# Last stage of a two-layer graph network: own values as transposes, ranks by one maximum, and the edge product moved from GpSimd to VectorE

## The chip, the cores and the metric

One Trainium2 chip, one of its cores. The metric is the device time of one launch in microseconds (us), the median of several runs.

## What is computed

A node table x of 50,000 rows by 256 features goes through two graph layers. The edges are 25,000 random pairs plus one self loop for each node. The first layer is a two-layer perceptron with a batch norm and a degree-weighted sum over edges. The second is attention with 8 heads of 32 features over the same edges:

```python
h = jnp.maximum(_layernorm(x, axis=-1), 0.0)
q = (x @ Wq + bq).reshape(n, DH, H) * scaling
k = (x @ Wk + bk).reshape(n, DH, H)
v = (x @ Wv + bv).reshape(n, DH, H)
s = jnp.einsum('edh,edh->eh', q[row], k[col])
m = jax.ops.segment_max(s, row, num_segments=n)
e = jnp.exp(s - m[row])
z = jax.ops.segment_sum(e, row, num_segments=n)
a = e / z[row]
out = jax.ops.segment_sum(a[:, None, :] * v[col], row, num_segments=n)
return out.reshape(n, -1) @ Wo + bo
```

`x` in the five lines for q, k and v is `h`, and the result is added to x. All arrays are fp32.

## The kernel before

The kernel runs in stages, each a loop over 98 tiles of 512 nodes (`TILE`; 128 partitions by 4 rows, `ROWS`). The stages ahead sort the edges, compute the first layer, and write q, k, v, the scores of the self loops and the weights that go with them to tables. The change lies in the last stage, whose names begin with `e_`, and in a constant made at the start.

In the last stage every tile has at most 512 slots for its true edges. For each tile GpSimd gathers the far node's keys and values (`e_kv`, four indirect DMAs of 128 rows), and SyncE loads the tile's own values (`e_mine`), queries (`e_q`), self state (`e_state`) and rows of x (`e_x`). A one-hot matrix from slots to nodes, `hot_h`, is built by VectorE (L2290), turned by TensorE (L2228), and widened to fp32 by ScalarE. With it TensorE spreads the queries over the slots (L2256), brings scores to the nodes (L2265) and attention weights back to the slots (L2244). A slot's place among the edges of its node is its rank. It is found with a product by the upper triangle `before_h` (L2232) and four multiply-and-add instructions (L2335), and `e_layer` holds it as a one-hot of 8.

The attention-weighted mean is accumulated in `e_mean_ps`, in two halves of the features (`kc`), for four rows each: the gathered values times their weight (L2138, GpSimd) by `hot` (L2216), and the own values times theirs (L2191, ScalarE, 32 instructions of one row and head) by the fp32 identity (L2218). An fp32 matmul written once in the code stands twice in the trace. ScalarE copies the mean out (L2183), TensorE multiplies by the output weights (L2204, L2206), VectorE adds x (L2282), and SyncE stores.

Each engine runs its own program over a ring of tiles (`over_ring`). In turn i, `at(l)` is tile i - l, so that in one turn TensorE works on tile i (turn, prefix, queries), i-1 (scores), i-2 (edge weights), i-3 (mean) and i-4 (output). The order within a turn is written out by hand, and the engines meet at semaphores alone. TensorE's order is: turn and prefix, first half of the output (`product(at(4), 0)`), `mean(at(3), 0)`, second half of the output, edge weights, `mean(at(3), 1)`, queries, scores. VectorE's turn begins with `hot_h` of tile i, then `e_seen` of tile i-2, which waits for TensorE's scores of the turn before.

The mean and GpSimd's product before:

```python
for j in range(ROWS):
    nc.tensor.matmul(mean_ps[kc][...], kv[w][:, j, ...], hot[w][:, j, :], start=True, stop=False)
    last = nc.tensor.matmul(mean_ps[kc][...], mine[w][:, j, ...], ident[:, :], start=False, stop=True)
```

## Time and profile before

| what | value |
|---|---|
| median of 3 runs (lowest, highest) | 3628.44 us (3624.29, 3637.78) |
| span of the profiled execution, first to last instruction | 3555.4 us |
| median less span | 73.0 us |
| TensorE busy, share of the span | 3183.0 us, 90% |
| VectorE busy | 2914.9 us, 82% |
| ScalarE busy | 2651.2 us, 75% |
| GpSimd busy | 1969.9 us, 55% |
| last stage, first `e_hot_h` to the end of the span | 2408.8 to 3555.4 us |

The profile shows one execution. Its span leaves out what lies before the first and after the last instruction. No time of its own is given for that execution beside the span, so the time is compared through the 73.0 us. A busy share over the whole span mixes stages, and a stage's limit is read in a window of its own.

### The profile page before, as it was taken

The page shows a single profiled execution, that of the slowest core. Times are in us where ns is not written, and L with a number is a line of the kernel's source. Part 1 is how long each engine was busy: PE and PEld are TensorE (multiplying, and loading weights), DVE is VectorE, ACT ScalarE, POOL GpSimd, SP SyncE. Part 2 cuts the span into 40 slices and gives each one's busy share as a digit, 9 for nine tenths or more (in the row PEclk, how much of TensorE's full clock was granted, in tenths as well). Part 3 has the DMA queues.
Part 4 walks back from the last instruction along what each step waited for, and adds up shares of the span by engine and source line. Part 5 has one row for each costly group of instructions (what it writes and reads, how often), then busy time and mean ns, then how long its engine had stood idle before and what let it go on. Part 6 is the DMA issues. An engine that isn't in the chain of part 4 may idle for free. (4 is left out here: it accounts for less than half of the span.)

```text
span 3555.4 us, 83958 instructions
## 1 busy us (share of the span) xinstructions
PE 3183.0 (90%) x21026; PEld 2603.3 (73%) x21026; DVE 2914.9 (82%) x8060; ACT 2651.2 (75%) x7851; POOL 1969.9 (55%) x1669
## 2 busy tenths in 40 slices
PE   1699999699998289999999999947999999999998
PEld 0355554477776278888888888836999999999998
DVE  8788887588875378888888888847999999999996
ACT  0688888599997467777777777726888888888886
POOL 0344444155554387777777777725555555555552
PEclk6799999899999689999999999978999999999999
DMA  1455555488886478888888888737666666666663
GB/s 33 145 203 203 201 201 193 175 306 308 307 306 253 166 265 309 310 309 309 308 308 309 308 309 308 290 125 237 236 232 232 232 237 234 233 232 234 233 237 110
DMA packets 335632, 861.24 MB, mean 242 GB/s; under 512 B 98483, under 2 KB 152922, under 8 KB 323018
## 3 DMA queue, kind: packets, MB, share of 16 engines
q1 hardware_dynamic: 241082, 678.75, 53.4%
q0 software_dynamic: 66256, 78.94, 7.5%
q10 hardware_dynamic: 28224, 102.77, 7.1%
q8 instruction: 25, 0.41, 0.0%
q14 instruction: 45, 0.37, 0.0%
HBM read 521.95 MB, written 416.52 MB: 264 GB/s over the span
## 5 line engine op out<-in xcount | busy, mean ns | idle before, releaser
L2191 ACT ACTIVATE e_mine<-e_mine,e_attention 128x32 f32<-128x32 f32 x3136 | 684.8, 308 | 57.8 <-DVE e_attention L2329 57.5
L1715 PE MATMUL c_qkv_ps<-w_qkv_lo,c_ht_hi 128*128 128x256 f16 x2352 | 642.0, 273 | 0.0
L1715 PE MATMUL c_qkv_ps<-w_qkv_hi,c_ht_hi 128*128 128x256 f16 x2352 | 642.0, 273 | 0.0
L1715 PE MATMUL c_qkv_ps<-w_qkv_hi,c_ht_lo 128*128 128x256 f16 x2352 | 641.9, 273 | 0.0
L2146 POOL DMA_INDIRECT e_kv<-kv_table,e_near x392 | 420.9, 1074 | 127.9 <-issue 100.8
L1607 POOL DMA_INDIRECT c_got<-y_table,c_near x392 | 395.0, 1008 | 110.0 <-issue 95.1
L2138 POOL TENSOR_TENSOR e_kv<-e_kv,e_part_of 128x1024 f32<-128x1024 f32 x98 | 188.2, 1921 | 411.2 <-DVE e_part_of L2352 411.2
L2206 PE MATMUL e_out_ps<-w_out,e_mean_t 128*128 128x256 f32 x1568 | 392.8, 380 | 0.0
L776 POOL DMA_INDIRECT dst_slots<-dst_word,dst_goal x240 | 236.6, 986 | 267.5 <-ACT a_hn L812 189.9
L846 PE MATMUL a_h_ps<-a_ht,w_t 128*128 128x512 f32 x784 | 360.8, 603 | 25.1 <-ACT h L794 21.5
L1109 PE MATMUL mix_ps<-w_mix,hb 128*128 128x256 f32 x1568 | 358.1, 382 | 21.2 <-ACT hb L1078 21.2
L1319 POOL DMA_INDIRECT src_slots<-staged_word,staged_goal x240 | 233.1, 971 | 252.2 <-DVE sort_lane_hot L1205 178.4
L1109 PEld LDWEIGHTS mix_ps<-w_mix,hb 128*128 128x128 f32 x1568 | 297.0, 191 | 68.0 <-ACT hb L1078 25.6
L2216 PE MATMUL e_mean_ps<-e_hot,e_kv 128*128 128x128 f32 x1568 | 309.1, 279 | 4.4 <-issue 2.6
L2218 PE MATMUL e_mean_ps<-ident,e_mine 128*128 128x128 f32 x1568 | 304.1, 276 | 0.0
L1600 POOL TENSOR_TENSOR c_x<-c_agg,c_x 128x1024 f32<-128x1024 f32 x98 | 231.1, 2358 | 127.9 <-ACT c_agg L1644 116.1
L2206 PEld LDWEIGHTS e_out_ps<-w_out,e_mean_t 128*128 128x128 f32 x1568 | 267.4, 191 | 44.4
L1702 PE MATMUL c_sum_ps<-c_got,c_sum_hot 128*128 128x256 f32 x784 | 218.8, 403 | 75.3 <-DVE c_agg L1767 47.5
L846 PEld LDWEIGHTS a_h_ps<-a_ht,w_t 128*128 128x128 f32 x784 | 141.4, 190 | 187.9 <-issue 187.9
L1655 ACT ACTIVATE c_hn<-c_x,c_shift,c_rstd 128x256 f32<-128x256 f32 x392 | 203.4, 589 | 95.8 <-DVE c_shift L1788 95.8
L2216 PEld LDWEIGHTS e_mean_ps<-e_hot,e_kv 128*128 128x128 f32 x1568 | 246.0, 192 | 10.4 <-issue 3.5
L1592 POOL TENSOR_TENSOR c_qk<-c_q,c_kv 128x1024 f32<-128x1024 f32 x98 | 232.5, 2373 | 34.8 <-DVE c_kv L1752 32.6
(425 smaller groups left out, 8143.7 us busy)
## 6 DMA issues: line engine op xcount, KB each, us to landing
kv_table<-c_kv SPq DMA_DIRECT2D x98, 1024.0 KB, 6.7
h_table<-h ACTq DMA_DIRECT2D x98, 512.0 KB, 2.6
h<-h_table SPq DMA_DIRECT2D x98, 512.0 KB, 4.2
y_table<-y_out ACTq DMA_DIRECT2D x98, 512.0 KB
agg_table<-agg_out SPq DMA_DIRECT2D x98, 512.0 KB
c_agg<-agg_table SPq DMA_DIRECT2D x98, 512.0 KB, 4.3
x_table<-c_x SPq DMA_DIRECT2D x98, 512.0 KB, 2.7
q_table<-c_q SPq DMA_DIRECT2D x98, 512.0 KB, 4.2
```

The lines of the kernel that those rows point to most:

```text
L776: nc.gpsimd.indirect_dma_start(out=dst_slots, out_offset=bass.IndirectOffsetOnAxis(ap=dst_goal[:, k:k + 1], axis=0), in_=dst_word[:, k:k + ...
L846: last = nc.tensor.matmul(h1_ps[:, oc * TILE:(oc + 1) * TILE], w1_t[:, kc, oc * P:(oc + 1) * P], ht[u][:, kc, :], start=kc == 0, stop=kc = ...
L1109: last = nc.tensor.matmul(mix_ps[u][:, j * D:(j + 1) * D], hb[u][:, kc, j * P:(j + 1) * P], w_mix[:, kc, :], start=kc == 0, stop=kc == KC - 1)
L1319: nc.gpsimd.indirect_dma_start(out=src_slots, out_offset=bass.IndirectOffsetOnAxis(ap=staged_goal[h][:, k:k + 1], axis=0), in_=staged_word ...
L1592: nc.gpsimd.tensor_tensor(qk[u][:, :, :], qb[w][:, :, :], kv[w][:, :, 0, :], ALU.mult).then_inc(qk_ready, 1)
L1607: nc.gpsimd.indirect_dma_start(out=got[w][:, j, :], out_offset=None, in_=y_table, in_offset=bass.IndirectOffsetOnAxis(ap=near[w][:, j:j + ...
L1715: last = nc.tensor.matmul(qkv_ps[n][:, j * D:(j + 1) * D], h[u][:, kc, j * P:(j + 1) * P], wt[:, kc, n * D:(n + 1) * D], start=m == 0, sto ...
L2146: nc.gpsimd.indirect_dma_start(out=kv[w][:, j, :], out_offset=None, in_=kv_table, in_offset=bass.IndirectOffsetOnAxis(ap=near[w][:, j:j + ...
L2191: last = nc.scalar.activation(of_head, of_head, ACT.Copy, scale=attention[u][:, j, h, 0:1])
L2206: last = nc.tensor.matmul(out_ps[:, j, :], mean_t[u][:, kc, row * P:(row + 1) * P], w_out[:, kc, :], start=False, stop=kc == KC - 1)
L2216: nc.tensor.matmul(mean_ps[kc][:, j * P:(j + 1) * P], kv[w][:, j, D + kc * P:D + (kc + 1) * P], hot[w][:, j, :], start=True, stop=False)
L2218: last = nc.tensor.matmul(mean_ps[kc][:, j * P:(j + 1) * P], mine[w][:, j, kc * P:(kc + 1) * P], ident[:, :], start=False, stop=True)
```

## The change

- TensorE: in `mean`, the four own values come first, each as a transpose (`is_transpose=True`) into the accumulation, and then the four products of the gathered values. The wait for the gathered values stands between the two. The prefix is taken with `raised_h` in place of `before_h`: the upper triangle with 256 on the diagonal, made by three more instructions on GpSimd at the start.
- VectorE: the rank is one maximum over the prefix (a slot's own node gives 256 plus its rank), compared with lanes 256 to 263. The floor of 0.5 under the total is gone. The last of four rows of own values is multiplied by VectorE (L2338 after), and so is the whole edge product (L2373 after). `hot_h` is built one turn ahead and later in the turn, and `layered` directly behind the scores.
- ScalarE: 24 multiplications of own values in place of 32.
- GpSimd: only the gathers are left.

```diff
-                    if at(3) is not None:
-                        t, (w, n) = ring_tile(at(3)), in_ring(at(3), RING)
-                        s = in_ring(at(3), SHORT)[0]
-                        hold(pool, part_ready, t + 1)
-                        value = kv[w][:, :, D:2 * D].rearrange("p r (h d) -> p r h d", h=H)
-                        nc.gpsimd.tensor_tensor(value, value, part_of[s][:, :, :].unsqueeze(3).to_broadcast([P, ROWS, H, DH]),
-                                                ALU.mult).then_inc(shared, 1)
...
-                            for j in range(kc * 2, kc * 2 + 2):
+                            for j in range(kc * 2, min(kc * 2 + 2, ROWS - 1)):
...
                 def mean(at, kc):
                     t, w = ring_tile(at), in_ring(at, RING)[0]
-                    pe.wait_ge(shared, t + 1)
                     pe.wait_ge(own_shared, t * 2 + 2)
+                    pe.wait_ge(own_last, t + 1)
                     wait_past(pe, mean_t_ready, t * 2 + (kc - 1))
                     for j in range(ROWS):
-                        nc.tensor.matmul(mean_ps[kc][:, j * P:(j + 1) * P], kv[w][:, j, D + kc * P:D + (kc + 1) * P], hot[w][:, j, :],
-                                         start=True, stop=False)
-                        last = nc.tensor.matmul(mean_ps[kc][:, j * P:(j + 1) * P], mine[w][:, j, kc * P:(kc + 1) * P],
-                                                ident[:, :], start=False, stop=True)
+                        nc.tensor.matmul(mean_ps[kc][:, j * P:(j + 1) * P], mine[w][:, j, kc * P:(kc + 1) * P], ident[:, :],
+                                         start=j == 0, stop=False, is_transpose=True, skip_group_check=True)
+                    pe.wait_ge(shared, t + 1)
+                    for j in range(ROWS):
+                        last = nc.tensor.matmul(mean_ps[kc][:, j * P:(j + 1) * P], kv[w][:, j, D + kc * P:D + (kc + 1) * P], hot[w][:, j, :],
+                                                start=False, stop=True, skip_group_check=True)
                     last.then_inc(mean_ready, 1)
...
-                            last = nc.tensor.matmul(prefix_ps[:, j, :], before_h[:, :], hot_h[s][:, j, :], start=True, stop=True)
+                            last = nc.tensor.matmul(prefix_ps[:, j, :], raised_h[:, :], hot_h[s][:, j, :], start=True, stop=True)
...
+                    own = mine[w][:, ROWS - 1, :].rearrange("p (h d) -> p h d", h=H)
+                    v.tensor_tensor(own, own, attention[u][:, ROWS - 1, :, 0].unsqueeze(2).to_broadcast([P, H, DH]),
+                                    ALU.mult).then_inc(own_last, 1)
...
-                        v.tensor_scalar(total[u][:, :, :], total[u][:, :, :], 0.5, None, ALU.max).then_inc(totalling, 1)
...
-                        for j in range(ROWS):
-                            last = v.scalar_tensor_tensor(counted[u][:, j, :], prefix_ps[:, j, :], 1.0, hot_h[s][:, j, :], ALU.mult, ALU.mult,
-                                                          accum_out=rank[u][:, j:j + 1])
-                        last.then_inc(ranked, 1)
...
+                    v.reduce_max(rank[u][:, :], prefix_ps[:, :, :], axis=AX.X).then_inc(ranked, 1)
...
+                def share(at):
+                    t, w, s = ring_tile(at), in_ring(at, RING)[0], in_ring(at, SHORT)[0]
+                    dve.wait_ge(part_ready, t + 1)
+                    value = kv[w][:, :, D:2 * D].rearrange("p r (h d) -> p r h d", h=H)
+                    v.tensor_tensor(value, value, part_of[s][:, :, :].unsqueeze(3).to_broadcast([P, ROWS, H, DH]),
+                                    ALU.mult).then_inc(shared, 1)
...
-                over_ring(dve, NT, 0, 4, step)
+                over_ring(dve, NT, 1, 4, step)
```

VectorE before, in the loop of the last stage, from the attention weights to `hot_h` of the next tile:

```order
L2329 TENSOR_TENSOR e_attention<-e_weight,e_inverse 128x288
...
L2335 SCALAR_TENSOR_TENSOR e_counted,e_rank<-e_prefix_ps,e_hot_h 128x128 x4
L2339 TENSOR_TENSOR e_layer<-lane,e_rank 128x32
L2344 TENSOR_REDUCE e_score<-e_qk 128x32
L2348 TENSOR_TENSOR e_of_edge<-e_small_ps,e_layer 128x256
L2352 TENSOR_REDUCE e_part_of<-e_of_edge 128x32
L2358 TENSOR_TENSOR e_layered<-e_score,e_layer 128x256
...
L2282 TENSOR_TENSOR e_x_3<-e_out_ps,e_x_3 128x512
...
L2290 TENSOR_TENSOR e_hot_h<-lane,slot_lane 128x512
```

The same stretch of VectorE after the change:

```order
L2333 TENSOR_TENSOR e_attention<-e_weight,e_inverse 128x288
L2338 TENSOR_TENSOR e_mine<-e_mine,e_attention 128x256
L2354 TENSOR_REDUCE e_score<-e_qk 128x32
L2358 TENSOR_TENSOR e_layered<-e_score,e_layer 128x256
...
L2344 TENSOR_REDUCE e_rank<-e_prefix_ps 128x4
L2348 TENSOR_TENSOR e_layer<-lane,e_rank 128x32
...
L2294 TENSOR_TENSOR e_hot_h<-lane,slot_lane 128x512
L2364 TENSOR_TENSOR e_of_edge<-e_small_ps,e_layer 128x256
L2367 TENSOR_REDUCE e_part_of<-e_of_edge 128x32
...
L2287 TENSOR_TENSOR e_x_3<-e_out_ps,e_x_3 128x512
L2373 TENSOR_TENSOR e_kv<-e_kv,e_part_of 128x4x256
```

`e_layered` has moved up behind the scores, the ranks are one instruction and come after, `hot_h` stands ahead of the edge weights, and the turn ends with the edge product `e_kv`, which GpSimd had.

TensorE after, from the edge weights to the queries (a row's x4 counts what the code writes; an fp32 matmul becomes two in the trace):

```order
L2249 MATMUL e_small_ps<-e_attention,e_hot_t 128x64 x4
L2219 MATMUL e_mean_ps<-ident,e_mine 128x128 x4
L2223 MATMUL e_mean_ps<-e_hot,e_kv 128x128 x4
L2257 ISA
L1357 ISA
L2261 MATMUL e_q_ps<-e_q,e_hot_t 128x256 x4
```

The same mean before had its eight in turns, one of the gathered and one of the own values for each row:

```order
L2216 MATMUL e_mean_ps<-e_hot,e_kv 128x128
L2218 MATMUL e_mean_ps<-ident,e_mine 128x128
L2216 MATMUL e_mean_ps<-e_hot,e_kv 128x128
L2218 MATMUL e_mean_ps<-ident,e_mine 128x128
L2216 MATMUL e_mean_ps<-e_hot,e_kv 128x128
```

The own values now all stand ahead of the gathered ones.

## Rows read from the trace of the kernel before

PE is TensorE, DVE VectorE, ACT ScalarE, POOL GpSimd. An arrow in brackets names what ended an idle time.

**Rows 1.** Windows: stretch, length, busy time per engine (instructions), PEclk, DMA share, GB/s

```profile
1800.00:2100.00 300.00, 289.00 (x2373) 251.79 (x2374) 258.93 (x566) 219.36 (x591) 235.37 (x162) 1.00 0.84 309
3000.00:3200.00 200.00, 200.00 (x1479) 185.63 (x1479) 182.31 (x453) 169.57 (x692) 109.95 (x89) 1.00 0.67 232
```

**Rows 2.** Chain that ended last, 3000 to 3040 us, by line

```profile
by line: PE e_out_ps L2206 28.1%; PE e_q_ps L2256 17.3%; PE e_mean_ps L2216 16.2%; PE e_mean_ps L2218 15.6%; PE e_small_ps L2265 8.4%; PE e_small_ps L2244 6.3%; PE e_out_ps L2204 3.8%; PE e_turn_ps L2228 2.2%; PE e_prefix_ps L2232 2.2%
```

**Rows 3.** Timeline of PE, one turn: start, length, instruction, count

```profile
3004.19 0.39 PE L2228 MATMUL e_turn_ps<-ident_h,e_hot_h 128*128 128x128 f16 x4
...
3006.58 0.38 PE L2216 MATMUL e_mean_ps<-e_hot,e_kv 128*128 128x128 f32 x2
3006.80 0.39 PE L2218 MATMUL e_mean_ps<-ident,e_mine 128*128 128x128 f32 x2
...
3008.37 0.27 PE L2204 MATMUL e_out_ps<-b_out,all_b 128*128 128x256 bf16 x1
...
3010.32 1.00 PE L2244 MATMUL e_small_ps<-e_attention,e_hot_t 128*128 128x64 f32 x8
...
3015.56 0.39 PE L2228 MATMUL e_turn_ps<-ident_h,e_hot_h 128*128 128x128 f16 x4
```

**Rows 4.** Timeline of DVE, the same turn

```profile
3004.61 0.42 DVE L2296 TENSOR_TENSOR e_seen<-e_small_ps,absent 128x256 f32<-128x256 f32 x1 [0.67 <-PE e_small_ps L2265]
...
3007.13 0.68 DVE L2282 TENSOR_TENSOR e_x<-e_out_ps,e_x 128x512 f32<-128x512 f32 x1
3007.73 0.20 DVE L2319 TENSOR_TENSOR e_weight<-e_weight,e_state 128x32 f32<-128x32 f32 x1
...
3009.66 0.28 DVE L2335 SCALAR_TENSOR_TENSOR e_counted<-e_prefix_ps,e_hot_h 128x128 f16<-128x128 f32 x1
...
3010.61 0.19 DVE L2339 TENSOR_TENSOR e_layer<-lane,e_rank 128x32 f32<-128x32 f16 x1
...
3013.57 1.80 DVE L2290 TENSOR_TENSOR e_hot_h<-lane,slot_lane 128x512 f16<-128x512 f16 x1
3016.01 0.42 DVE L2296 TENSOR_TENSOR e_seen<-e_small_ps,absent 128x256 f32<-128x256 f32 x1 [0.64 <-PE e_small_ps L2265]
```

**Rows 5.** Timeline of POOL, the same turn

```profile
3012.91 1.92 POOL L2138 TENSOR_TENSOR e_kv<-e_kv,e_part_of 128x1024 f32<-128x1024 f32 x1 [4.12 <-DVE e_part_of L2352]
```

**Rows 6.** By source line: count, ns min/median/max, first and last start

```profile
L2290 DVE TENSOR_TENSOR e_hot_h<-lane,slot_lane x98: 628/1801/2401, 2408.8 to 3502.3; 128x512 f16<-128x512 f16 x98
...
L2304 DVE TENSOR_TENSOR e_below<-e_seen,e_peak x98: 457/458/1524, 2425.5 to 3526.4; 128x288 f32<-128x288 f32 x98
...
L2296 DVE TENSOR_TENSOR e_seen<-e_small_ps,absent x98: 424/425/426, 2424.6 to 3525.5; 128x256 f32<-128x256 f32 x98
```

**Rows 7.** Timeline of DVE and of POOL at the start of the stage

```profile
2432.14 0.69 DVE L2290 TENSOR_TENSOR e_hot_h<-lane,slot_lane 128x512 f16<-128x512 f16 x1
...
2431.96 1.14 POOL L2146 DMA_INDIRECT e_kv<-kv_table,e_near  x1 [0.30 <-issue]
```

**Rows 8.** DVE groups by shape: busy us, mean ns

```profile
L1184 DVE TENSOR_TENSOR mix<-mix_ps,b_mix 128x1024 f32<-128x1024 f32 x98 | 119.8, 1222 | 83.9 <-ACT agg_out L1092 54.8 <-PE mix_ps L1109 29.0 <-issue 0.2
L2344 DVE TENSOR_REDUCE e_score<-e_qk 128x32 f32<-128x1024 f32 x98 | 118.8, 1212 | 0.0
...
L2301 DVE TENSOR_REDUCE e_peak<-e_seen 128x32 f32<-128x288 f32 x98 | 44.4, 453 | 3.4
...
L2358 DVE TENSOR_TENSOR e_layered<-e_score,e_layer 128x256 f32<-128x256 f32 x98 | 40.7, 415 | 0.0
...
L2323 DVE TENSOR_SCALAR e_total<-e_total 128x32 f32<-128x32 f32 x98 | 27.2, 278 | 3.4
```

**Rows 9.** Timeline of PE in the stage ahead: transposes and what follows

```profile
2101.95 0.60 PE L1690 MATMUL c_turn_ps<-ident,c_hn 128*128 128x128 f32 x4
2102.38 0.27 PE L1715 MATMUL c_qkv_ps<-w_qkv_hi,c_ht_hi 128*128 128x256 f16 x1
```

**Rows 10.** Timeline of ACT, the same turn

```profile
3009.77 3.50 ACT L2191 ACTIVATE e_mine<-e_mine,e_attention 128x32 f32<-128x32 f32 x16 [0.60 <-DVE e_attention L2329]
```

More of the change, by code:

```diff
@@ L54 @@
 HIST = 6
+RAISE = 256
 PEAKS, WEIGHTS = 0, H
@@ L243, in build @@
         before_h = sb("before_h", [P, P], F16)
+        raised_h = sb("raised_h", [P, P], F16)
         spare = sb("spare", [P, 3])
@@ L2033, in build @@
             hot_t = [sb(f"e_hot_t{w}", [P, ROWS, P], where=part) for w in short]
-            counted = [sb(f"e_counted{u}", [P, ROWS, P], F16, where=part) for u in two]
             rank = [sb(f"e_rank{u}", [P, ROWS], where=part) for u in two]
@@ L2089, in build @@
             own_shared = sem("e_own_shared")
+            own_last = sem("e_own_last")
             shared = sem("e_shared")
@@ new lines, in slot_hot @@
+                def slot_hot(at):
+                    t, s = ring_tile(at), in_ring(at, SHORT)[0]
+                    if not isinstance(t, int) or t >= SHORT:
+                        hold(dve, hot_ready, t - (SHORT - 1))
+                        hold(dve, prefix_ready, t - (SHORT - 1))
+                    v.tensor_tensor(hot_h[s][:, :, :], lane[:, 0:P].unsqueeze(1).to_broadcast([P, ROWS, P]),
+                                    slot_lane[:, bass.ds(t * ROWS, ROWS)].unsqueeze(2).to_broadcast([P, ROWS, P]),
+                                    ALU.is_equal).then_inc(hot_h_ready, 1)
@@ new lines, in peaks @@
+                def peaks(at):
+                    t, u = ring_tile(at), at[1] % 2
+                    dve.wait_ge(seen_ready, t + 1)
+                    v.tensor_tensor(seen[u][:, :, :, 1:LAYERS + 1], seen_ps.rearrange("p (r h l) -> p r h l", h=H, l=LAYERS),
+                                    absent[:, bass.ds(t * ROWS, ROWS), :].unsqueeze(2).to_broadcast([P, ROWS, H, LAYERS]),
+                                    ALU.add).then_inc(masked, 1)
+                    dve.wait_ge(masked, t + 1)
+                    dve.wait_ge(own_seen, t + 1)
+                    v.reduce_max(peak[u][:, :, :], seen[u][:, :, :, :], axis=AX.X).then_inc(peak_ready, 1)
+                    dve.wait_ge(peak_ready, t + 1)
+                    wait_past(dve, weight_ready, t - 1)
+                    v.tensor_tensor(below[u][:, :, :, :], seen[u][:, :, :, :],
+                                    peak[u][:, :, :].unsqueeze(3).to_broadcast([P, ROWS, H, LAYERS + 1]), ALU.subtract).then_inc(below_ready, 1)
@@ new lines, in products @@
+                def products(at):
+                    t, (w, n) = ring_tile(at), in_ring(at, RING)
+                    dve.wait_ge(kv_landed[w], n * 64 + 64)
+                    for half in two:
+                        dve.wait_ge(q_ready, t * 2 + (half + 1))
+                        v.scalar_tensor_tensor(qk[:, half * 2:half * 2 + 2, :], q_ps[half][:, :, :], SCALE,
+                                               kv[w][:, half * 2:half * 2 + 2, 0:D], ALU.mult, ALU.mult).then_inc(qk_ready, 1)
@@ new lines, in scores @@
+                def scores(at):
+                    t, s, u = ring_tile(at), in_ring(at, SHORT)[0], at[1] % 2
+                    dve.wait_ge(qk_ready, t * 2 + 2)
+                    v.reduce_sum(score[u][:, :, :], qk[:, :, :].rearrange("p r (h d) -> p r h d", h=H), axis=AX.X).then_inc(score_ready, 1)
+                    dve.wait_ge(score_ready, t + 1)
+                    dve.wait_ge(layer_ready, t + 1)
+                    wait_past(dve, seen_ready, t - 1)
+                    v.tensor_tensor(layered[u][:, :, :, :], score[u][:, :, :].unsqueeze(3).to_broadcast([P, ROWS, H, LAYERS]),
+                                    layer[s][:, :, :].unsqueeze(2).to_broadcast([P, ROWS, H, LAYERS]), ALU.mult).then_inc(layered_ready, 1)
@@ L2353, in step @@
[L2353 to L2359 removed]
+                        normalise(at(2))
@@ L2360, in step @@
+                    if at(1) is not None:
+                        scores(at(1))
+                    if at(0) is not None:
+                        ranks(at(0))
+                    if at(-1) is not None:
+                        slot_hot(at(-1))
+                    if at(2) is not None:
+                        parts(at(2))
                     if at(4) is not None:
                         result(at(4), 1)
-                over_ring(dve, NT, 0, 4, step)
+                    if at(2) is not None:
+                        share(at(2))
```

109 lines of the change are left out of this document (44 added, 65 removed).

## The prediction

> **What bounds the kernel now.** The change touches the last stage, so I read the windows of that stage first, not the page's shares. In the stretch from 3000 to 3200 us TensorE is busy for all 200.00 us at a granted clock of 1.00, VectorE for 182.31, ScalarE for 169.57, GpSimd for 109.95, and the DMA engines for 0.67 of the time [rows 1]. Then the chain of waits: over the sampled 40 us, every share is TensorE's, and L2218, the own values by the identity, has 15.6% of it [rows 2]. TensorE is therefore the bound, and its turn is read from one `e_turn` to the next: 3015.56 - 3004.19 = 11.37 us [rows 3].
>
> Next comes who is close behind. VectorE's turn goes from `e_seen` to `e_seen`, 3004.61 to 3016.01. Its last instruction, `hot_h`, ends at 3013.57 + 1.80 = 3015.37, and then it waits 0.64 us for TensorE's scores [rows 4]. So it has 10.76 us of work in a turn of 11.40: when TensorE gets shorter by more than 0.64 us, VectorE takes over, unless its own work shrinks too. The change adds work there, so the number that matters is VectorE's new sum.
>
> The count of turns: 98 `e_seen` between 2424.6 and 3525.5, 97 distances of 11.35 us on average [rows 6].
>
> **TensorE's sum.** One mean (both parts of four rows) takes 3008.37 - 3006.58 = 1.79 us for 16 passes, 0.112 each; two passes are one fp32 matmul, as the two entries x2 show [rows 3]. The own values are 8 of them, 0.895 us. The stage ahead transposes fp32 blocks of the same 128x128 against the same identity, and there four stand in the trace as four, not eight, and what follows starts 0.43 us later [rows 9]. A mean thus saves 0.895 - 0.43 = 0.465 us and a turn, with two means, 0.93. TensorE's own work becomes 11.37 - 0.93 = 10.44 us. Nothing hides this gain, as TensorE has no idle time. What is not shown is a transpose that opens an accumulation; the lower bound is that of the row, the upper one the two passes of an ordinary fp32 matmul, thus no gain. I take the row, being the same instruction on the same shapes. The new triangle has the same shape and type as the old, so it costs the same.
>
> The Trainium skill speaks against the transposes (TensorE: Matmul & The Clock Gate, part 4, PE-mode transpose): transpose mode does not count as busy work for the clock gate. The trace disagrees as far as it can: the stretch from 1800 to 2100 us holds such transposes in every tile and has a granted clock of 1.00 [rows 1]. At half the clock of this stage, 1.2 in place of 2.4 GHz, its 10.44 us would be near 20.9, and the time near 4,550 us. I give this 1 in 100.
>
> **VectorE's sum.** I start from 10.76 us and change it piece by piece. Two rules of thumb from the rows: an instruction that depends on nothing just ahead starts 0.08 us before that one's end (3007.73 against 3007.13 + 0.68) [rows 4], and one that waits for its direct predecessor starts 0.035 us after it (idle 3.4 us over 98) [rows 8]. A new dependence so costs 0.115.
>
> - The floor under the total goes: 0.278 + 0.035 = 0.31 less [rows 8].
> - The four rank instructions take 3010.61 - 3009.66 = 0.95 [rows 4]. In their place stands one maximum over 512 columns. Reductions of 288 and 1024 columns take 0.453 and 1.212 us [rows 8], 1.03 ns a column, so 512 are 0.684, with the wait 0.72. That is 0.23 less; with the two rows themselves as bounds, 0.46 less to 0.30 more.
> - Own values of one row: 256 columns at 0.415 [rows 8], less the 0.08, and a wait on the attention weights of 0.115: 0.45 more.
> - `layered` right behind the scores that it needs: 0.115 more.
> - The edge product, 1024 columns: the nearest instruction of that size on VectorE takes 1.222 [rows 8], so 1.14 more after the overlap. GpSimd needed 1.92 for it [rows 5]; that is the upper bound.
> - `hot_h`. Its 1.80 us are not work. GpSimd's product runs from 3012.91 to 3014.83 [rows 5], `hot_h` starts inside it and ends 0.54 us after its end, at 3015.37 [rows 4]. The smallest `hot_h` of the stage takes 0.628 us [rows 6], and one that ran with no GpSimd product about takes 0.69 [rows 7]. With the product gone from GpSimd, `hot_h` is worth 0.69 - 0.08 = 0.61: 1.19 less.
>
> The sum: 10.76 - 0.31 - 0.23 + 0.45 + 0.115 + 1.14 - 1.19 = 10.73 us. The move to VectorE thus nearly pays for itself, because the old place made VectorE stand still for most of what the product costs it now.
>
> The Trainium skill has this as a rule (SBUF — State Buffer, two separate sides): VectorE and GpSimd have one pair of ports in common, the one that starts first keeps it for its whole instruction, and a VectorE instruction with two SBUF inputs blocks only against a GpSimd one that reads SBUF. The trace agrees on the blocked `hot_h`. What the page leaves open for this case is whether a gather on GpSimd counts as such a read: then `hot_h` and the new product would wait for gathers. In the rows `hot_h` takes 0.69 us while a gather runs from 2431.96 for 1.14 us [rows 7], and `e_below`, also of two SBUF inputs, has a median of 0.458 against a minimum of 0.457 [rows 6]. It is the gather that gives way.
>
> **The loop through both engines.** The second half of the output needs room that VectorE's first `e_x` makes. From `e_seen` to the end of that `e_x` are 3007.81 - 3004.61 = 3.20 us [rows 4]; from there TensorE does the second half of the output to the scores, 3015.56 - 3008.37 = 7.19 [rows 3], now 6.73; and VectorE's `e_seen` begins 0.45 after the next turn's start (3016.01 - 3015.56). Together 10.38, and one handover from VectorE to TensorE that no row shows apart. Between 0 and the 0.45 of the other handover, I take 0.15: 10.53. This circle lies 0.2 below VectorE's sum, so it can only add a little. The edge weights are safer: the attention weights are ready at 3009.74 (0.08 behind 3009.66), 5.13 after `e_seen`, now 4.82, with the 0.45 at 5.27 in TensorE's turn; TensorE gets to them at 3010.32 - 3004.19 = 6.13, now 5.67 [rows 3, 4].
>
> **What costs nothing.** ScalarE loses 8 of 32 multiplications, 16 of which take 3.50 us [rows 10]; that is 1.75 us off an engine that had waits, so it brings nothing. GpSimd has only gathers left. They are queued behind no product, and what they wait for is the mean of six tiles before. The wait that VectorE's product brings into `mean` stands behind the transposes, and the product ends with VectorE's turn, while TensorE's first mean is 3006.58 - 3004.19 = 2.39 us into its own. If VectorE were late by more than about 2 us there, the mean would wait. At the start three small instructions are added on GpSimd ahead of everything; from 1.92 us for 1024 columns [rows 5] 128 columns are 0.24, together 0.7 us.
>
> **Sum.** The longest of 10.73 (VectorE), 10.53 (circle) and 10.44 (TensorE) sets the turn. 97 x (11.35 - 10.73) = 60.1 us. The last turns, which drain the ring behind the last `e_seen`, have two more turns' worth of transposes with TensorE in the lead, 2 x 0.93 = 1.9. The median of the runs is 73.0 us above the profiled span, and I take that as unchanged: 3628.4 - 60.1 - 1.9 + 0.7 = 3567 us, a span of 3494.
>
> **Rivals.**
>
> 1. VectorE's sum is too high (a cheaper maximum, no gap where I put one) and TensorE stays the bound at 10.44: 3628.4 - 97 x 0.91 - 1.9 + 0.7 = 3539 us. For it: my gaps are averages, and the missing 0.3 us is little. Against: the edge product's 1.14 is a firm row. 14 in 100, with the stretch down to about 10.55.
> 2. The engines catch on each other: sum and circle are within 0.2 us, and a handover of 0.45 brings the circle to 10.83; a delay on one is then no longer taken up on the other. At 11.1 a turn: 3628.4 - 97 x 0.25 - 1.2 = 3603 us. 14 in 100.
> 3. Nothing gained: the transpose in an accumulation takes two passes, TensorE keeps its 11.37, and VectorE's 10.73 hides behind it: 3629 us. 6 in 100.
> 4. Slower: `hot_h` keeps its 1.80, or as much is lost when the new product and it stand behind a gather, which now fall together. VectorE's turn is then 10.73 + 1.19 = 11.92: 3628.4 + 97 x 0.57 - 1.2 = 3682 us. It decides once VectorE loses more than 0.62 us a turn, and passes the 0.5% at 0.81. Against it stand the rows above on gathers. 5 in 100, and 1 for the clock.
>
> The forecast, a turn of 10.55 to 10.9, has 60 in 100 and its own range from 3550 to 3583.
>
> **How the numbers follow.** A measurement of this kernel tells about 0.5%, 18 us, from no change. Faster by more than that: the forecast and rivals 1 and 2, 88 in 100. Within it: rival 3, 6. Slower: rival 4 and the clock, 6. The range takes in most of rivals 1 and 2: 3541 to 3600.
>
> **What would show it.** Right: `e_turn` to `e_turn` near 10.7 us, VectorE with no idle before `e_seen`, TensorE with small waits for VectorE, `hot_h` at 0.63 to 0.69, the maximum near 0.68, the edge product near 1.22, eight single transposes a turn in 0.86 us. Wrong: idle on VectorE before `e_seen` with TensorE full (rival 1), waits on both (rival 2), own values still twice each in the trace (rival 3), `hot_h` or the product above 1.5 us (rival 4).

## The result, and the profile after

The changed kernel takes 3614.4 us (median of 20 runs, 3608.13 to 3655.64), the kernel before beside it 3631.98 (20 runs). The ratio is 0.9959 with a 95% interval of 0.9943 to 0.9974: 17.6 us gained where 61 were forecast, and a time above the forecast range of 3541 to 3600.

The runs fell on several chips, and these differ: on some of them the kernel before takes 3615 to 3639 us, on others 3556, steadily within each; the times shown at first are of the former, and the profile shown at first, with its span of 3555.4 us, fits the latter only. I call them slower and faster chips. The 73.0 us between median and span were thus the difference of two chips and not a constant: every execution's time is its span and 1.7 to 2.1 us. The result above and the profile of after are of a slower chip; the profiled execution took 3636.14 us, 22 more than the median.

The windows, of the changed kernel, with the columns of [rows 1]:

```profile
1800.00:2100.00 300.00, 281.91 (x2297) 241.80 (x2295) 252.66 (x548) 213.30 (x575) 228.84 (x158) 1.00 0.82 300
3000.00:3200.00 200.00, 179.54 (x1284) 159.55 (x1283) 176.46 (x338) 136.13 (x525) 69.89 (x69) 1.00 0.68 223
```

TensorE, full before, now has 20 us of idle in 200, VectorE 24: neither is the bound by its work. The clock is unchanged at 1.00.

By source line, with the columns of [rows 6]:

```profile
L2294 DVE TENSOR_TENSOR e_hot_h<-lane,slot_lane x98: 629/692/694, 2440.8 to 3587.1; 128x512 f16<-128x512 f16 x98
...
L2373 DVE TENSOR_TENSOR e_kv<-e_kv,e_part_of x98: 1212/1217/1282, 2478.4 to 3616.9; 128x1024 f32<-128x1024 f32 x98
...
L2344 DVE TENSOR_REDUCE e_rank<-e_prefix_ps x98: 681/683/693, 2442.6 to 3596.9; 128x4 f32<-128x512 f32 x98
...
L2301 DVE TENSOR_TENSOR e_seen<-e_small_ps,absent x98: 409/416/425, 2461.9 to 3609.6; 128x256 f32<-128x256 f32 x98
```

These instructions have the length that the prediction gave them: `hot_h` 0.69, product 1.217, maximum 0.683. But the turn, (3609.6 - 2461.9) / 97 = 11.83 us, is longer than the 11.35 of [rows 6], and the stage begins 37 us later than there, although the stages ahead are unchanged.

The waits from 2500 to 3400 us (engine, waiting instruction, who released it: us in all, times, longest):

```profile
ACT e_mean_t L2186 <- PE e_mean_ps L2223: 106.6, 76, 2.0
...
PE e_out_ps L2207 <- DVE e_x L2287: 92.3, 72, 1.7
DVE e_x L2287 <- remote: 54.6, 60, 1.1
```

TensorE waits in 72 of some 76 turns for VectorE's first `e_x`, and that `e_x` itself waits in 60 for a releaser that this view cannot name ("remote"). One such turn shows why. PE, then ACT, DVE and POOL, four timelines of the same stretch:

```profile
3007.90 0.39 PE L2233 MATMUL e_turn_ps<-ident_h,e_hot_h 128*128 128x128 f16 x4
...
3009.43 1.03 PE L2209 MATMUL e_out_ps<-w_out,e_mean_t 128*128 128x256 f32 x4
3010.30 0.60 PE L2219 MATMUL e_mean_ps<-ident,e_mine 128*128 128x128 f32 x4
3010.74 1.06 PE L2223 MATMUL e_mean_ps<-e_hot,e_kv 128*128 128x128 f32 x8
3013.25 0.28 PE L2207 MATMUL e_out_ps<-b_out,all_b 128*128 128x256 bf16 x1 [1.46 <-DVE e_x L2287]
...
3020.20 0.39 PE L2233 MATMUL e_turn_ps<-ident_h,e_hot_h 128*128 128x128 f16 x4
```

```profile
3010.11 0.60 ACT L2167 ACTIVATE e_hot_t<-e_turn_ps 128x512 f32<-128x512 f16 x1 [1.62 <-remote]
```

```profile
3010.35 1.28 DVE L2317 SCALAR_TENSOR_TENSOR e_qk<-e_q_ps,e_kv 128x512 f32<-128x512 f32 x2
3012.50 0.69 DVE L2287 TENSOR_TENSOR e_x<-e_out_ps,e_x 128x512 f32<-128x512 f32 x1 [0.87 <-remote]
```

```profile
3007.72 1.00 POOL L2149 DMA_INDIRECT e_kv<-kv_table,e_near  x1 [0.30 <-issue]
3009.03 1.00 POOL L2149 DMA_INDIRECT e_kv<-kv_table,e_near  x1 [0.30 <-issue]
3010.33 1.00 POOL L2149 DMA_INDIRECT e_kv<-kv_table,e_near  x1 [0.30 <-issue]
```

TensorE turns `hot_h` at 3007.90 for 0.39 us, and what it queues next runs on at once. ScalarE's `e_hot_t` needs only that result, but starts at 3010.11, 2.2 us later, after 1.62 of waiting. The first output ends at about 3010.46 (an end that the profile models), and `e_x`, for which VectorE is free at 3011.63, starts at 3012.50. So it is not TensorE's next work that is late but the news of the work done, the semaphore event that releases the other engines, and this happens while GpSimd issues gathers. Without the product ahead of them the four gathers of a turn begin about 1.4 us before it. The turn takes 12.30 us.

The trace also holds the semaphore events themselves, which the views above leave out. In this turn the event of `e_turn` stands at 3010.00 and that of the first output at 3012.38: `e_hot_t` starts 0.11 and `e_x` 0.12 us behind its event. So the unnamed releaser is TensorE's own event. The delay of `e_hot_t` is an extreme: over the turns from 2500 to 3400 us it starts 0.71 us behind TensorE's turn in the median and 2.23 at most. The delay of the first `e_x` is the rule: it starts 4.59 us behind the turn's start in the median.

### The profile page after: what moved, and what is told of

Its sections match the earlier page's. It is cut to its first block and busy times, and to the rows that moved or that the text cites. A ratio compares the mean times of both kernels' runs of the same rounds, so it can differ in the third digit from the quotient of the medians.

```text
span 3634.4 us, 80654 instructions
## 1 busy us (share of the span) xinstructions
PE 3110.7 (86%) x20242; PEld 2488.1 (68%) x20242; DVE 2932.1 (81%) x7472; ACT 2500.9 (69%) x7067; POOL 1777.4 (49%) x1574
## 5 line engine op out<-in xcount | busy, mean ns | idle before, releaser
L2149 POOL DMA_INDIRECT e_kv<-kv_table,e_near x392 | 413.1, 1054 | 738.5 <-issue 698.2
L2194 ACT ACTIVATE e_mine<-e_mine,e_attention 128x32 f32<-128x32 f32 x2352 | 518.7, 308 | 149.5 <-DVE e_attention L2333 149.5
L1725 PEld LDWEIGHTS c_qkv_ps<-w_qkv_lo,c_ht_hi 128*128 128x128 f16 x2352 | 230.1, 98 | 26.8
L1725 PEld LDWEIGHTS c_qkv_ps<-w_qkv_hi,c_ht_lo 128*128 128x128 f16 x2352 | 230.1, 98 | 26.5
L1725 PEld LDWEIGHTS c_qkv_ps<-w_qkv_hi,c_ht_hi 128*128 128x128 f16 x2352 | 230.1, 98 | 24.4
L1762 DVE SCALAR_TENSOR_TENSOR c_kv<-c_qkv_ps,unscale,b_qkv 128x1024 f32<-128x1024 f32 x196 | 242.2, 1275 | 3.4 <-PE c_qkv_ps L1725 3.4
```

The costliest lines, as they stand in the source:

```text
L1725: last = nc.tensor.matmul(qkv_ps[n][:, j * D:(j + 1) * D], h[u][:, kc, j * P:(j + 1) * P], wt[:, kc, n * D:(n + 1) * D], start=m == 0, sto ...
L1762: v.scalar_tensor_tensor(goes, qkv_ps[n][:, :].rearrange("p (j d) -> p j d", j=ROWS), unscale[:, 0:1], b_qkv[:, n * D:(n + 1) * D].unsquee ...
L2149: nc.gpsimd.indirect_dma_start(out=kv[w][:, j, :], out_offset=None, in_=kv_table, in_offset=bass.IndirectOffsetOnAxis(ap=near[w][:, j:j + ...
L2194: last = nc.scalar.activation(of_head, of_head, ACT.Copy, scale=attention[u][:, j, h, 0:1])
```

## The experiments

**Theory.** Two losses stand between forecast and result: VectorE's own chain is longer than 10.73 us, and completions of TensorE reach the others late when gathers are issued near them, which costs time at the start of its turn, where the new order leaves no slack. **Rivals.** VectorE's length with the product is the whole loss; the product itself collides with the gathers; SyncE's store or loads, not the gathers, delay the news.

### The change in parts

`e1_before_again` is the kernel before, for its trace on a slower chip.

> The kernel of before, unchanged, to see how far one profile speaks for the timed runs: the first profile had a span of 3555.4 us, while the runs lie near 3632. Theory A (before, too, has turns in which TensorE and VectorE stand still, and the first profile happened to have none): a span near 3630 and turns of the last stage between 11.4 and 12.3 us. Theory B (before always keeps 11.38 us and only the stages ahead vary): a span near 3630 with all turns at 11.38. Ratio to before 1.000 within 0.3% either way.

3632.85 us, ratio 0.9998 (0.9985 to 1.0011). Its `e_seen`, x98, start from 2467.6 to 3601.0 us: a turn of 11.69 us, not 11.35. The kernel before has some longer turns on such a chip too; from `e_turn` at 2927.00 to the next at 2939.07 are 12.07. Both theories of the expectation hold in part: the turns are longer (A), and the stage also begins 2467.6 - 2424.6 = 43 us later (B).

`e2_transposes_alone`, on the kernel before:

```diff
                     for j in range(ROWS):
-                        nc.tensor.matmul(mean_ps[kc][:, j * P:(j + 1) * P], kv[w][:, j, D + kc * P:D + (kc + 1) * P], hot[w][:, j, :],
-                                         start=True, stop=False)
...
+                        nc.tensor.matmul(mean_ps[kc][:, j * P:(j + 1) * P], mine[w][:, j, kc * P:(kc + 1) * P], ident[:, :],
+                                         start=j == 0, stop=False, is_transpose=True, skip_group_check=True)
+                    pe.wait_ge(shared, t + 1)
...
```

> Before, with the own values as transposes that open the accumulation, and nothing else. By the sums, TensorE falls to 10.44 us a turn and VectorE's 10.76 takes over: a turn near 10.8, 97 x 0.55 = 53 us less, ratio 0.985. Theory of the collision (the loss comes from gathers that run while SyncE issues loads and VectorE multiplies): the gathers stay where they were, so the gain comes in full, 0.985. Rival (any TensorE below its bound meets the same stalls): ratio 0.995 or above.

3582.62 us, ratio 0.9858 (0.984 to 0.9877), as expected. By source line and, in the second fence, the waits from 2500 to 3400 us:

```profile
L2291 DVE TENSOR_TENSOR e_hot_h<-lane,slot_lane x98: 629/1801/2400, 2445.8 to 3531.1; 128x512 f16<-128x512 f16 x98
```

```profile
PE e_turn_ps L2229 <- DVE e_hot_h L2291: 32.4, 81, 0.6
```

The transposes alone gain nearly three times what the whole change gains. Then TensorE waits for `hot_h`, still 1.8 us long beside GpSimd's product. The turn is (3552.3 - 2469.6) / 97 = 11.16 us, not the expected 10.8; the ratio fits because it started from 11.69.

`e3_product_on_gpsimd` is the changed kernel with only the product moved back, ahead of the gathers:

```diff
# GpSimd
+                    if at(3) is not None:
...
+                        nc.gpsimd.tensor_tensor(value, value, part_of[s][:, :, :].unsqueeze(3).to_broadcast([P, ROWS, H, DH]),
+                                                ALU.mult).then_inc(shared, 1)
                     if at(-2) is not None:
...
# VectorE
-                    if at(2) is not None:
-                        share(at(2))
```

> The changed kernel with the edges' product back on GpSimd, at its old place ahead of the gathers; all else as changed. VectorE loses 1.14 us of product; hot_h stands ahead of the edge weights now, so it need not meet the product. Sums: VectorE 9.6 to 10.0, TensorE 10.44: a turn of 10.5 if the collision is gone with the gathers' old place (ratio 0.977). Rival (the loss is not due to where gathers or product run): a turn near 11.8, ratio 0.995.

3506.14 us (3504.76 to 3508.76), ratio 0.9651 (0.9636 to 0.9666): the best of all, 108 us under the changed kernel's 3614.4 (both on slower chips, with 3632.37 and 3631.98 us for the kernel before). It had been expected at 0.977. Its window, `hot_h` by source line, and one turn on DVE, POOL and PE:

```profile
3000.00:3200.00 200.00, 200.00 (x1455) 182.34 (x1454) 178.84 (x364) 152.27 (x592) 115.36 (x96) 1.00 0.73 254
```

```profile
L2301 DVE TENSOR_TENSOR e_hot_h<-lane,slot_lane x98: 627/693/694, 2442.3 to 3455.8; 128x512 f16<-128x512 f16 x98
```

```profile
3006.75 0.69 DVE L2301 TENSOR_TENSOR e_hot_h<-lane,slot_lane 128x512 f16<-128x512 f16 x1 [0.25 <-issue]
```

```profile
3008.41 1.91 POOL L2148 TENSOR_TENSOR e_kv<-e_kv,e_part_of 128x1024 f32<-128x1024 f32 x1 [3.42 <-DVE e_part_of L2375]
3010.47 1.14 POOL L2156 DMA_INDIRECT e_kv<-kv_table,e_near  x1 [0.15 <-issue]
```

```profile
3019.53 0.39 PE L2240 MATMUL e_turn_ps<-ident_h,e_hot_h 128*128 128x128 f16 x4
...
3029.95 0.22 PE L2240 MATMUL e_turn_ps<-ident_h,e_hot_h 128*128 128x128 f16 x1
```

TensorE is full again at 10.42 us in this turn, 0.02 from the predicted sum of 10.44, and at 10.49 over all 97. And `hot_h` takes 0.69 us with the product on GpSimd: in the new order of VectorE it stands ahead of `e_part_of`, which the product waits for, so the two never meet. The new order alone is enough to free `hot_h`; the move was not needed for it. The gathers now begin 1.6 us behind TensorE's turn (3010.47 against 3008.88).

`e8_row_on_scalar` takes e3 and gives ScalarE the last row of own values back (`min(kc * 2 + 2, ROWS - 1)` is `kc * 2 + 2` again, VectorE's multiplication L2338 is gone).

> The kernel with the product back on GpSimd, and the own values' last row back on ScalarE too. VectorE loses 0.43 us a turn and ScalarE gains 0.88, both beside TensorE, which is busy all the time there (10.42 us a turn): 3500-3512 us, as with the row on VectorE. If ScalarE's later e_mine holds the opening transposes: up to 3550 us.

3537.09 us, ratio 0.9724 (0.9707 to 0.974), 31 us more than e3, against the first expectation and within the second (up to 3550). The two runs are of two chips. By the turns, (3508.4 - 2464.5) / 97 = 10.76 against 10.49, the difference is 97 x 0.27 = 26 us. In the waits from 2500 to 3400 us TensorE's weight load for the opening transposes waits in 27 turns for ScalarE's multiplications and in 57 with no releaser named, which e3 does not have:

```profile
PEld e_mean_ps L2225 <- issue: 26.6, 57, 1.7
...
PEld e_mean_ps L2225 <- ACT e_mine L2201: 10.9, 27, 0.4
```

From TensorE's turn to the gathered values of the first mean are 3009.84 - 3006.78 = 3.06 us, in e3 3011.71 - 3008.88 = 2.83. So ScalarE, busy 177.66 of 200 us in the window at 3000, is late with the own values, as the second expectation had it. The move of that row, which the prediction costed at nothing on ScalarE's side, is worth some 26 us once the product is back on GpSimd.

### Where the gathers are

`e4_gathers_later` adds one line ahead of the gathers:

```diff
                             hold(pool, mean_ready, (t - RING) * 2 + 2)
+                            hold(pool, attention_ready, t - 3)
```

> The changed kernel with one wait more on GpSimd: the gathers of a tile start only behind the attention weights of the tile four before, so about 5 us into TensorE's turn and not at its end, clear of SyncE's loads (0.7 to 2.8 us into the turn) and of most of VectorE's product. Theory of the collision: TensorE's completions no longer come late, a turn near 11.0 as in the undisturbed turns of the first profile, ratio 0.985 to before. Rival (the place of the gathers does not matter): ratio 0.995 as the changed kernel.

3648.11 us, ratio 1.004 (1.0026 to 1.0053). It was meant to free the turn's start, but the fourth gather falls on the next one. POOL, PE and ACT:

```profile
3006.28 1.00 POOL L2150 DMA_INDIRECT e_kv<-kv_table,e_near  x1 [0.30 <-issue]
```

```profile
3006.46 0.39 PE L2234 MATMUL e_turn_ps<-ident_h,e_hot_h 128*128 128x128 f16 x4
```

```profile
3008.39 0.60 ACT L2168 ACTIVATE e_hot_t<-e_turn_ps 128x512 f32<-128x512 f16 x1 [1.24 <-remote]
```

The fourth gather lies over the turn's start, and `e_hot_t` waits 1.24 us; over the turns from 2500 to 3400 us it starts 1.92 us behind `e_turn` in the median. The expectation (0.985) failed.

`e5_gathers_between` has `hold(pool, below_ready, t - 3)` in that place. The other two leave work out, so their output is not the kernel's: `e6_no_gathers` has no gathers and no waits for them, and `e7_no_product` has no `share` on VectorE (TensorE waits for `part_ready` in its place).

> The changed kernel, its four gathers held until VectorE has written e_below of the tile four before, so that the first starts about 1.5 us after TensorE begins a turn, where it starts in the kernel with the product back on GpSimd. Theory 'signals' (TensorE's completion of the prefix sums reaches the others 4 us late because gathers are under way just then, and the turn has no slack for it there): the gathers no longer lie over the prefix sums, the turn falls from 11.9 to 11.0-11.3 us, and the time to 3535-3560 us. Theory 'length' (VectorE's own work with the product, 11 us, and its small gaps are the whole loss, wherever the gathers are): 3605-3625 us.

> The changed kernel without the four gathers of keys and values in each turn (keys and values stay zero, so this work is left out; every instruction on VectorE, ScalarE and TensorE stays). Theory 'signals': no completion is late, VectorE is never stopped, the turn is its undisturbed 11.0 us: 3530-3545 us. A theory that SyncE's own loads and stores make the signals late: 3600-3620 us. If VectorE's product alone is slow through something else, the turn stays over 11.5.

> The changed kernel with the product of the edges' values left out altogether (TensorE waits for e_part_of in its place), gathers where they were. VectorE has 9.8 us a turn. Theory 'signals, whatever VectorE does': the late signals stay (the prefix over 2 us late in most turns) but have over 1 us of slack: TensorE bound, 10.4 to 10.8 us a turn, 3505-3545 us. Theory 'VectorE's product lies over a gather and blocks it' : no late signal is left in the trace, the turn is 10.4 us, 3500-3510 us.

| | us | ratio, 95% | turn | first gather behind the turn's start |
|---|---|---|---|---|
| e5 | 3574.15 | 0.9826, 0.981 to 0.9843 | 11.17 | 3009.12 - 3005.65 = 3.5 |
| e6 | 3549.64 | 0.9761, 0.9745 to 0.9778 | 11.02 | none |
| e7 | 3657.93 | 1.006, 1.0043 to 1.0076 | 12.03 | under way at the start |

(Turns are the distance from the first to the last `e_seen`, divided by 97.) The waits of e7 from 2500 to 3400 us, and then those of e5:

```profile
DVE e_x L2287 <- remote: 118.3, 72, 1.9
...
PE e_out_ps L2207 <- DVE e_x L2287: 103.2, 71, 1.7
```

```profile
PE e_out_ps L2208 <- DVE e_x L2288: 32.8, 78, 0.5
```

e7 decides against two rivals at once. VectorE has 1.2 us a turn less to do, and the kernel is slower than before; so VectorE's length is not the whole loss. And the late news stays without the product, so it is no collision of VectorE's product with a gather. In e5 all work is there, only the gathers start later, and no wait of `e_x` or `e_hot_t` is left in the trace. e5 came out 14 us above its expected band; e6 agrees in the turn, but was 5 us above its band as well.

e7 was wrong for every theory in its size: 10.8 us a turn at most had been expected, with slack for the news. The trace shows where that slack was missing. A turn with late news is as long with the product as without it: distances of `e_turn` over 11.5 us have a median of 12.19 in the changed kernel and of 12.18 in e7, since both wait for the first output and not for VectorE's work. The changed kernel has 60 such turns of 76, e7 73. Why e7 has more is not known.

The semaphore events show the late news directly. The table has the time from the start of the last matmul of a group to its event, in us, as the median over the turns from 2500 to 3400 us (a few events are missing in the traces):

| | chip | turn | prefix | first output | first mean | second output | second mean |
|---|---|---|---|---|---|---|---|
| changed kernel | slower | 0.52 | 3.95 | 2.30 | 0.99 | 0.39 | 0.29 |
| e7, no product | slower | 0.52 | 3.98 | 2.41 | 1.10 | 0.39 | 0.29 |
| e4, gathers later | slower | 1.71 | 1.54 | 0.39 | 0.29 | 0.39 | 0.63 |
| e5, gathers between | slower | 0.23 | 0.23 | 0.39 | 0.29 | 0.39 | 1.03 |
| e3, product on GpSimd | slower | 0.23 | 0.23 | 0.39 | 0.83 | 2.02 | 0.29 |
| e6, no gathers | slower | 0.23 | 0.23 | 0.39 | 0.29 | 0.39 | 0.29 |
| e17, changed kernel (below) | faster | 0.23 | 0.23 | 0.39 | 0.29 | 0.39 | 0.29 |

Without gathers every event has its shortest time. With them some events of the turn are late, and which ones follows the gathers' place. e3 and e5 have late events too, but theirs release work that has slack, while the first output has none. The kernel before also has a late first output on a slower chip, 1.69 us in e1, which goes with its longer turns.

### Store, loads or gathers

`e9_small_store` stores 16 of 1024 values of each row and leaves out the rest of the output. `e10_loads_later` has one more wait ahead of SyncE's loads, `e11_gathers_at_hot_t` holds the gathers by another signal, and `e12_before_gathers_between` is the kernel before with the line of e5:

```diff
# e10, SyncE
                         wait_past(sp, mean_ready, (t - RING) * 2 + 2)
+                        wait_past(sp, qk_ready, (t - 3) * 2 + 2)
# e11, GpSimd
                             hold(pool, mean_ready, (t - RING) * 2 + 2)
+                            hold(pool, hot_t_ready, t - 1)
```

> The changed kernel with the last stage's store cut to the first 16 of the 1024 values of each row of a tile (the rest of the output is left out), everything else as it was. The gathers stay over the opening of TensorE's turn. Theory 'store': the signals are late because the gathers meet the 0.5 MB store that SyncE issues at the turn's start: the turn falls to 11.0-11.2 us and the time to 3530-3555 us. Theory 'gathers' (wherever a gather starts under those signals they are late, whatever else moves): the turn stays near 11.8 and the time at 3590-3625 us.

> The changed kernel with SyncE's four loads of a turn held until VectorE has written the second half of e_qk of the tile three before, some 4 us after TensorE begins a turn, after most of the gathers; only the store is still issued at the turn's start. Theory 'loads' (SyncE issues three loads between the gathers, and the two hold each other and TensorE's signals up): the turn falls to 11.0-11.2 us, 3540-3560 us. Theory 'gathers': 3595-3625 us.

> The changed kernel with its gathers held until ScalarE has written e_hot_t of the tile two before, about 1.2 us into TensorE's turn: the place that they have in the kernel with the product back on GpSimd, behind the turn's and the prefix sums' signals and over those of the first product and the first mean. If only the signals at the turn's opening have no slack: as with the gathers held for e_below, 3565-3585 us. If a gather does as much harm over the first product's signal, which lets VectorE write e_x: 3595-3625 us.

> The kernel before with its gathers held until e_below of the tile four before is written. In its profiled runs the gathers start 0.6 us ahead of TensorE's turn; in one run all turns took 11.38 us, in another one in three took 12.1 with a late signal. If the gathers' place is what costs the changed kernel, the kernel before loses its slow turns with it: 11.38 us a turn, 3595-3610 us. If not, 3625-3640 us.

This chip was a faster one (before: 3556.19 us): 3522.01, 3518.77 and 3518.99 us, ratios 0.9901, 0.9895 and 0.9892, and 3558.46 for e12 (1.0006, 0.9996 to 1.0015). No event of TensorE is late in any (medians of 0.23, 0.39 and 0.29 us as in e6), so the four say nothing on the cause. They were repeated beside the changed kernel.

> The changed kernel itself, beside the next three. On a chip on which the kernel before takes 3630-3640 us: 3608-3625 us, with late completions, as in its own runs. On a chip on which before takes 3556 us: theory 'late completions belong to the gathers' place on every chip': about 3590 us (ratio 1.01); theory 'they belong to chips of the slower kind': 3517-3525 us, 11.0-11.1 us a turn, VectorE's length, as the variants took there.

> The changed kernel with the last stage's store cut to the first 16 of the 1024 values of each row of a tile (the rest of the output is left out). Where the changed kernel beside it has late completions: 3560-3580 us if the store brings them about, 3605-3620 if not. Otherwise 3522 us again.

> The changed kernel with SyncE's four loads held until the second half of e_qk is written. Where the changed kernel beside it has late completions: 3560-3580 us if they need loads issued between the gathers, 3605-3620 if not. Otherwise 3519 us again.

> The changed kernel with its gathers held until e_hot_t of the tile two before is written. Where the changed kernel beside it has late completions: 3570-3585 us, as with the gathers held for e_below, if only the signals at the turn's opening have no slack; 3600-3620 if those of the first product count as much. Otherwise 3519 us again.

| | us | ratio, 95% | turn |
|---|---|---|---|
| e13, the changed kernel | 3609.72 | 0.998, 0.9965 to 0.9995 | 11.79 |
| e14, small store | 3604.51 | 0.9977, 0.9959 to 0.9996 | 11.82 |
| e15, loads later | 3605.02 | 0.9975, 0.9958 to 0.9992 | 11.85 |
| e16, gathers later | 3561.82 | 0.9846, 0.983 to 0.9863 | 11.11 |

A slower chip (before: 3615.48 us). Waits from 2500 to 3400 us of e13, where e16 has none of its kind:

```profile
DVE e_x L2287 <- remote: 45.6, 61, 1.0
```

Store and loads change the time by 5 us at most, within the spread of the runs; the gathers' place matters, by 3609.72 - 3561.82 = 48 us. The turns are those of the profiled executions, and the ones of e13, e14 and e15 took 3632, 3628 and 3629 us, 22 to 24 above their medians, that of e16 only 3. So the 48 us are the figure to use, and not the 97 x (11.79 - 11.11) = 66 of the turns. e16's gathers start 3011.52 - 3009.21 = 2.3 us behind TensorE's turn; the run came out 8 us under its expected 3570.

> The changed kernel itself. On a chip on which before takes 3556 us: 3517-3525 us if the late completions belong to chips of the slower kind, about 3590 us if not. On one of the slower kind: 3605-3620 us, as twice before.

> The kernel before with its gathers held until e_below of the tile four before is written. On a chip of the slower kind: 20-35 us under the kernel before, if the gathers' place is behind its turns of 12.1 us; the same time, if not. On one of the faster kind: 3558 us again, no difference.

A faster chip. e17: 3518.65 us, before 3556.05, ratio 0.9894 (0.9878 to 0.9911). e18: 3558.25, ratio 1.0006 (0.9997 to 1.0016), as e12; so whether another place of the gathers would rid the kernel before of its 12 us turns on slower chips was not seen. One turn of e17, on PE, ACT and POOL:

```profile
3008.15 0.39 PE L2233 MATMUL e_turn_ps<-ident_h,e_hot_h 128*128 128x128 f16 x4
...
3012.44 0.28 PE L2207 MATMUL e_out_ps<-b_out,all_b 128*128 128x256 bf16 x1 [0.40 <-DVE e_x L2287]
```

```profile
3008.65 0.60 ACT L2167 ACTIVATE e_hot_t<-e_turn_ps 128x512 f32<-128x512 f16 x1
```

```profile
3007.93 1.00 POOL L2149 DMA_INDIRECT e_kv<-kv_table,e_near  x1 [0.30 <-issue]
3009.24 1.00 POOL L2149 DMA_INDIRECT e_kv<-kv_table,e_near  x1 [0.30 <-issue]
```

The same kernel, gathers in the same place, and `e_hot_t` starts 0.50 us behind TensorE's turn, not 2.2. In the medians it is 0.60 against 0.71, and the first `e_x` starts 3.61 us behind the turn, not 4.59. VectorE is full here; its timeline:

```profile
3009.19 0.42 DVE L2301 TENSOR_TENSOR e_seen<-e_small_ps,absent 128x256 f32<-128x256 f32 x1
...
3013.57 0.46 DVE L2333 TENSOR_TENSOR e_attention<-e_weight,e_inverse 128x288 f32<-128x288 f32 x1 [0.19 <-DVE e_inverse L2328]
...
3016.71 0.19 DVE L2348 TENSOR_TENSOR e_layer<-lane,e_rank 128x32 f32<-128x32 f16 x1
3017.06 0.69 DVE L2294 TENSOR_TENSOR e_hot_h<-lane,slot_lane 128x512 f16<-128x512 f16 x1 [0.15 <-issue]
...
3019.05 1.27 DVE L2373 TENSOR_TENSOR e_kv<-e_kv,e_part_of 128x1024 f32<-128x1024 f32 x1
3020.25 0.41 DVE L2301 TENSOR_TENSOR e_seen<-e_small_ps,absent 128x256 f32<-128x256 f32 x1
```

The turn is 3020.25 - 3009.19 = 11.06 us, with no idle before `e_seen`.

## Why the prediction was wrong, step by step

- **TensorE's sum, 10.44 us: right.** Four transposes take 3010.74 - 3010.30 = 0.44 in place of 0.895, and e3 runs at 10.42. The granted clock stayed at 1.00 in e3's window with eight transposes in every turn. So the rule that the prediction weighed, that transposes do not count as busy for the clock gate (the Trainium skill, TensorE: Matmul & The Clock Gate, PE-mode transpose), cost nothing here.
- **VectorE's sum, 10.73: 0.33 too low.** The lengths were right, the gaps were not. From the start of `e_layer` to that of `hot_h` are 3017.06 - 3016.71 = 0.35 us, where the sum had 0.19 - 0.08 = 0.11. In [rows 4] `hot_h` follows a long `e_x` with no gap; now it stands behind an instruction of 0.19 us, and 0.15 to 0.26 are put down to issue. That its two waits and the slice chosen by a register are what takes this time, and that a longer instruction ahead would cover it, is argued and was not tried. The rest is 0.06 each before the attention weights and in the product. On a faster chip, where no event is late, this covers the whole miss: 37.4 us gained (3556.05 - 3518.65) of 61, and 97 x 0.33 = 32 more than covers the 24 that are missing. The last turns, behind the last `e_seen`, gave some of it back: 29.9 us before and 24.8 after, 5.1 less where the prediction had 1.9.
- **`hot_h`, 1.19 us less: right in size, but not owed to the move.** The prediction said that the move to VectorE nearly pays for itself, because the old place made VectorE stand still. e3 has the product on GpSimd and `hot_h` at 0.69 all the same, by the new order. The 1.2 us of product on VectorE bought nothing.
- **"What costs nothing": the step that failed.** GpSimd having only gathers left was costed at zero. Without the product ahead of them the gathers begin just ahead of TensorE's turn, and on slower chips the news of the prefix (3.95 us in place of 0.23) and of the first output (2.30 in place of 0.39) then comes late, in some turns also that of the turn itself. The prefix has slack. The first output's news releases `e_x`, which the second output needs, in the circle that the prediction itself had found to be within 0.2 us of the bound. The gathers' place costs 48 us in the runs (e13 against e16). With them moved, 53.7 of the forecast 61 us are there on a slower chip (3615.48 - 3561.82), though part of it is what the kernel before loses in its own longer turns. An estimate closes the sum on a slower chip: from 11.69 to the predicted 10.73 would be 97 x 0.96 = 93 us, with 1.9 for the last turns 95; less 32 for VectorE's gaps and 48 for the gathers leaves 15, and 17.6 were measured.
- **The constant 73.0 us: wrong.** It hid a change of chip. The turn of the kernel before was 11.69 us, not 11.35, on the kind of chip on which it was timed.
- **The rivals.** Rival 2 named the place, a delay on one engine no longer taken up on the other, and 11.1 us a turn, which e5, e16 and e17 have. It did not name what comes late, and on slower chips the changed kernel went beyond it, to 11.83. Rival 4 looked at the gathers, but expected that they hold up VectorE's own instructions, which they do not: `hot_h` has a median of 692 ns and 694 at most. Its turn of 11.92 is near the measured one by luck.
- **What stays open** is why a gather on GpSimd delays TensorE's completions, and why on some chips only. The Trainium skill (Perfetto Trace Analysis, Tensor Engine Instruction) says that the end in the profile is an estimate, and that the update is pushed after PSUM's acknowledgement and must then reach the other engines. The events, 2.30 us behind the last matmul of the first output in place of 0.39, fit a delay in one of these two stages; no run here tells them apart, and the page names no condition for it. Nor does a run tell whether the issuing on GpSimd or the transfers that it starts are to blame: e6 leaves out both.

## What to carry to other kernels

An order that keeps two engines' instructions apart can free a blocked one without moving the other; try the order first (e3, with the product left in place: 108 us under the kernel that moved it). When an engine loses work, ask what it will start earlier, and over whose signal: a gather over a completion without slack cost 48 us here. And compare the profiled execution's own time with the timed runs before a constant is made of the difference.

## What was unexpected of the hardware

- On slower chips GpSimd's gathers delay semaphore events of TensorE, with TensorE itself running on: 2.30 us in place of 0.39 behind the last matmul of the first output, 3.95 in place of 0.23 for the prefix. Without gathers (e6) no event is late; with other places of the gathers (e3, e4, e5) other events are. A gather over a completion is not enough: in e3 the first gather runs from 3010.47 to 3011.61 over the end of the first output at 3011.44, and `e_x` starts at 3011.83 with nothing late. In the changed kernel it is the fourth gather that lies over that end, and in e4 the fourth that lies over the turn's start; whether the number or the place counts was not tried.
- It is not seen on faster chips (e17, same kernel: every event as in e6). The chips differ by 59 to 83 us for the kernel before. In e1 against the first profile, 43 us of it lie ahead of this stage and 97 x (11.69 - 11.35) = 33 in its turns.
- VectorE does not start `hot_h` for 0.15 to 0.26 us behind a 0.19 us instruction, with nothing to wait for in the trace.
